# An attention and gated-scan kernel: the output projection in fp16 high and low parts, half a step to a step later

## The reference

```python
x = x + attn(layernorm(x))                  # per batch; inside attn: rms_norm, qkv = h @ w_qkv.T, rope on q and k
#   attn = softmax(mask(q k^T / 8)); out = attn @ v
#   return out @ w_out.T                    # [256,1024] @ [1024,128]: the output projection
z = layernorm(x)
for t in range(32):                         # the scan, c is [256,128]
    f = sigmoid(z[t] @ wf.T + c @ uf.T + bf);  i = sigmoid(z[t] @ wi.T + c @ ui.T + bi)
    g = tanh(z[t] @ wc.T + c @ uc.T + bc);     c = f * c + i * g
x = x + tanh(z @ wo.T + c @ uo.T + bo)
```

## Time and profile before

| | |
|---|---|
| median of 3 runs | 1133.13 us (1126.74 to 1135.27) |
| the profiled execution's own time | 1133.03 us |
| its span, first to last instruction | 1131.2 us |
| PE busy | 1080.3 us, 95% of the span |
| PE weight loads (PEld) | 813.6 us, 72% |
| DVE / ACT / POOL busy | 930.0 (82%) / 698.4 (62%) / 634.8 us (56%) |
| chain that ended last | PE 59%, DVE 16%, DMA 14% |
| granted TensorE clock, mean | 0.988 of 2.4 GHz |

### The profile page before, as it was taken

One profiled execution on the slowest core, in us unless ns is written; L12 is line 12 of the kernel. 1 busy time (PEld: TensorE's weight loads), 2 busy tenths in 40 slices (PEclk: granted clock), 3 DMA queues, 4 the chain that ended last, 5 costly groups with the idle time before them and its releaser, 6 DMA issues.

```text
span 1131.2 us, 47261 instructions
## 1 busy us (share of the span) xinstructions
PE 1080.3 (95%) x18443; PEld 813.6 (72%) x18443; DVE 930.0 (82%) x3305; ACT 698.4 (62%) x1575; POOL 634.8 (56%) x816
## 2 busy tenths in 40 slices
PE   3879999999999999999999999999999999999996
PEld 2457777777777776777777777677777777777784
DVE  5778888888888888888888888788888888888745
ACT  3556666666666666666666666666665666666644
POOL 3545665576565647656555665555565565556420
PEclk8889999999999999999999999999999999999999
DMA  6213343332333442233333233333323333332215
GB/s 204 95 62 112 111 115 114 115 95 89 111 111 114 115 114 90 90 111 115 115 115 115 83 100 115 107 114 115 115 78 98 114 115 111 108 112 92 68 36 150
DMA packets 78031, 120.52 MB, mean 107 GB/s; under 512 B 13041, under 2 KB 35954, under 8 KB 77682
## 3 DMA queue, kind: packets, MB, share of 16 engines
q1 hardware_dynamic: 68714, 111.20, 32.5%
q10 hardware_dynamic: 9096, 6.30, 2.1%
HBM read 41.56 MB, written 8.78 MB: 45 GB/s over the span
## 4 chain that ended last, share of the span: by engine, by line
PE 59%; DVE 16%; DMA 14%; SPq 4%; issue 3%; POOL 2%; ACT 1%; DVEq 0%; POOLq 0%
PE bank_pv L1142 11%; PE bank L1034 11%; DMA rope_c<-rope_b 10%; PE bank_st L1098 8%; PE bank_sum L1179 5%; PE bank_sum L1163 4%; DVE masked L809 4%; PE bank_sm L1073 4%; PE bank L1056 3%; DMA linv_scratch<-linv 3%; SPq L312 3%; DVE linv L832 2%; DVE rope_a L798 2%; PE bank L1281 2%; PE bank L1283 2%
## 5 line engine op out<-in xcount | busy, mean ns | idle before, releaser
L407 POOL TENSOR_TENSOR qk<-rope_a,rope_c 128x512 f32<-128x512 f32 x256 | 341.0, 1332 | 312.9 <-DMA rope_c<-rope_b 288.9
L809 DVE CUSTOM_DVE_ANT_0 masked<-bank_sm,mask_q 128x132 bf16<-128x132 f32 (+1 forms) x1024 | 307.1, 355 | 17.7 <-PE bank_sm L1073 17.2
L798 DVE TENSOR_TENSOR rope_a<-bank,cos 128x512 f32<-128x512 f32 x256 | 174.1, 680 | 130.1 <-PE bank L1034 83.7
L400 POOL TENSOR_TENSOR prob<-prob 128x264 f32<-128x264 f32 x256 | 210.8, 823 | 117.1 <-ACT prob L544 108.3
L529 ACT ACTIVATE qk_h<-qk 128x512 f16<-128x512 f32 x256 | 160.4, 627 | 172.2 <-POOL qk L407 171.7
L544 ACT ACTIVATE prob<-bank_st 128x784 f32<-128x784 f32 x256 | 209.3, 817 | 59.7 <-PE bank_st L1107 58.9
L1142 PE MATMUL bank_pv<-prob,v_sb 128*64 128x256 f32 (+1 forms) x2048 | 224.8, 340 | 0.6 <-DVE raw L825 0.6
L1098 PE MATMUL bank_st<-qk 64*64 64x256 f32 (+3 forms) x4096 | 186.3, 299 | 0.4 <-issue 0.2
L1098 PEld LDWEIGHTS bank_st<-qk 64*64 64x64 f32 x4096 | 167.7, 134 | 9.6 <-issue 1.3
L799 DVE TENSOR_TENSOR rope_b<-bank,sin 128x512 f32<-128x512 f32 x256 | 173.8, 679 | 0.0
L1142 PEld LDWEIGHTS bank_pv<-prob,v_sb 128*64 128x64 f32 x2048 | 124.3, 136 | 54.4 <-issue 0.9
(11 more groups left out here) (237 smaller groups left out, 1732.1 us busy)
## 6 DMA issues: line engine op xcount, KB each, us to landing
rope_c<-rope_b SPq DMA_DIRECT2D x512, 128.0 KB, 2.3
rinv<-linv_scratch SPq DMA_DIRECT2D x124, 256.0 KB, 4.8
out<-x_sb SPq DMA_DIRECT2D x16, 256.0 KB, 3.7
linv_scratch<-linv SPq DMA_DIRECT2D x62, 64.0 KB, 2.1
x_sb<-x ACTq DMA_DIRECT2D x28, 128.0 KB, 5.5
xt<-w_qkv_t ACTq DMA_DIRECT2D x1, 1024.0 KB, 5.3
v_end<-v_end_scratch SPq DMA_DIRECT2D x64, 8.0 KB
v_sb<-pm_v SPq DMA_DIRECT2D x63, 8.0 KB
```

The lines of the kernel that those rows point to most:

```text
L400: G.tensor_tensor(prob_2[:, s % 4, :, :], prob[:, s % 4, :, 0:NT - Q1], prob[:, s % 4, :, C0 + Q1:SCOL], ALU.add).then_inc(S["prob_added"], 1)
L407: G.tensor_tensor(qk[:, s, :].rearrange("p (u n) -> p u n", u=2)[:, :, 0:NT], rope_a[:, (NPAIR * j + s) % 3, :].rearrange("p (u n) -> p u ...
L798: V.tensor_tensor(rope_a[:, (NPAIR * j + s) % 3, :], proj_bank(j, s)[:, :], cos[:, :], ALU.mult)
L809: ins = V.tensor_tensor_reduce(masked[:, e, c0:c0 + n], ps_sm[:, e, c0:c0 + n], mask_q[:, c0:c0 + n], 1.0, LOWEST, ALU.add, ALU.max, top[: ...
```

## The change

`w_out` is kept as two fp16 matrices, `wo_hi` (the weights times 64, rounded) and `wo_lo` (what the rounding left). The normalised attention output is split in the same way into `y_hl`: ScalarE writes the high parts (`y_high`, a copy to fp16), GpSimd the low parts (`y_low`, a subtraction), a quarter of a batch at a time. `project_out` makes three fp16 matmuls (high by high, high by low, low by high) where one fp32 matmul was: 48 of 128 columns for a batch. The residual divides by 64. `y_hl` lies in the memory of `rinv`, so `spread_linv` now waits until the previous batch's projection is done.

The first half of the projection moves from step 5 to step 6, the second half from behind `project` in step 6 to the end of step 6. `residual`, `second_stats` move from step 6 to step 7, `second_norm` to step 0 of the next iteration, `transpose_xn` to the end of step 0 with its readers in step 1, `gates` to the ends of steps 1 and 2 and their `tanh` to steps 2 and 3. The last two batches keep a special order.

```diff
-        wo_sb = sb("wo_sb", [P, NPAIR, D], f32)
+        wo_hi = sb("wo_hi", [P, NPAIR, D], f16)
+        wo_lo = sb("wo_lo", [P, NPAIR, D], f16)
...
-        rinv = sb("rinv", [P, NPAIR, NT], f32)
+        y_hl = sb("y_hl", [P, 4, 2, 2 * NT], f16)
+        rinv = y_hl[:, :, :, :].rearrange("p n u m -> p (n u m)").bitcast(f32).rearrange("p (s n) -> p s n", s=NPAIR)
...
@@ SP, spread_linv
-                wait(sp, S["norm_done"], 4 * cj)
+                wait(sp, S["y_ready"], cj)
...
@@ POOL
+            def y_low(cj, par, n):
+                pool.wait_ge(S["y_hi_done"], 4 * cj + n + 1)
+                G.tensor_tensor(y_hl[:, n, 1, :].rearrange("p (s n) -> p s n", s=2), raw[:, par, 2 * n:2 * n + 2, :],
+                                y_hl[:, n, 0, :].rearrange("p (s n) -> p s n", s=2), ALU.subtract).then_inc(S["y_lo_done"], 1)
...
-                    if c and s == 7 and j < NB:
-                        rstd(j - 2)
+                    if s == 6 and c and j < NB:
+                        y_low(j - 2, p, 2)
+                        y_low(j - 2, p, 3)
...
                     if s >= 1 and a:
                         rope_add(j, s - 1)
+                    if s == 5 and c and j < NB:
+                        y_low(j - 2, p, 0)
+                        y_low(j - 2, p, 1)
+                    if s == 7 and c and j < NB:
+                        rstd(j - 2)
                     if b:
                         prob_add(j - 1, s)
...
@@ ACT
+                cast(A.activation(wo_hi[:, :, :].rearrange("p c d -> p (c d)"), o_raw, ACT.Copy, scale=WS))
...
+            def y_high(cj, par, n):
+                act.wait_ge(S["norm_done"], 4 * cj + n + 1)
+                A.activation(y_hl[:, n, 0, :].rearrange("p (s n) -> p s n", s=2), raw[:, par, 2 * n:2 * n + 2, :],
+                             ACT.Copy).then_inc(S["y_hi_done"], 1)
...
-                    elif s in (1, 2) and d and j - 3 < NB - 1:
-                        gate_tanh(j - 3, s - 1)
+                    elif s in (2, 3) and d and j - 3 < NB - 1:
+                        gate_tanh(j - 3, s - 2)
...
+                    if s == 5 and c and j <= NB:
+                        y_high(j - 2, p, 0)
+                        y_high(j - 2, p, 1)
                     if s == 5 and real(j + 1):
                         h_high(j + 1, 1 - p)
...
-                    if s == 7 and c and j < NB:
-                        second_norm(j - 2)
+                    if s == 0 and d and j <= NB:
+                        second_norm(j - 3)
...
@@ DVE
+                V.scalar_tensor_tensor(wo_lo[:, :, :].rearrange("p c d -> p (c d)"), o_raw, WS,
+                                       wo_hi[:, :, :].rearrange("p c d -> p (c d)"), ALU.mult,
+                                       ALU.subtract).then_inc(S["casts_dve"], 1)
...
+                    if s == 7 and c and j < NB:
+                        residual(j - 2)
                     if a:
                         rotate(j, s)
...
@@ PE, project_out
-                pe.wait_ge(S["norm_done"], 4 * cj + n + 1)
+                pe.wait_ge(S["y_lo_done"], 4 * cj + n + 1)
...
-                        last = T.matmul(y_out(cj)[:, q * D:(q + 1) * D], raw[:, par, s, q * P:(q + 1) * P], wo_sb[:, s, :],
...
+                        at = s % 2 * NT + q * P
+                        for i, (u, v) in enumerate(SPLIT):
+                            last = T.matmul(y_out(cj)[:, q * D:(q + 1) * D], y_hl[:, n, u, at:at + P], WO[v][:, s, :],
...
@@ PE, body
-                    if s in (5, 6) and c and j != NB:
+                    if s == 6 and c and j < NB:
+                        project_out(j - 2, p, 0)
+                        project_out(j - 2, p, 1)
+                    if s in (5, 6) and j == NB + 1:
                         project_out(j - 2, p, 2 * (s - 5))
                         project_out(j - 2, p, 2 * (s - 5) + 1)
...
+                    if s == 6 and c and j < NB:
+                        project_out(j - 2, p, 2)
+                        project_out(j - 2, p, 3)
                     if s in (2, 4, 7) and b:
                         sums(j - 1, (2, 4, 7).index(s))
+                    if s == 0 and d and j <= NB:
+                        transpose_xn(j, j - 3)
+                    if s in (1, 2) and d and j <= NB:
+                        gates(j, j - 3, s - 1)
```

More of the change, by code:

```diff
@@ L646, in body @@
                         load_batch(j + 4)
-                    if s == 0 and d and j != NB + 1:
+                    if s == (0 if j > NB else 1) and d and j != NB + 1:
                         xt_high(j - 3)
+                    if s == 1 and j == NB + 1:
+                        for n in range(4):
+                            y_high(j - 2, p, n)
                     if s == 1 and d and j - 3 == NB - 1:
                         gate_tanh_last(j - 3)
-                    elif s in (1, 2) and d and j - 3 < NB - 1:
-                        gate_tanh(j - 3, s - 1)
+                    elif s in (2, 3) and d and j - 3 < NB - 1:
+                        gate_tanh(j - 3, s - 2)
+                    if s == 3 and b:
+                        copy_top(j - 1, 1)
                     if s < 2 and j == 1:
@@ L691, in body @@
                         first_norm(j + 1)
+                    if s == 5 and c and j <= NB:
+                        y_high(j - 2, p, 2)
+                        y_high(j - 2, p, 3)
                     if s == 5 and d:
@@ L1310, in body @@
                             out_cf(g)
-                    elif s == 0 and d and j <= NB:
-                        transpose_xn(j, j - 3)
-                    if s in (1, 2) and d and j <= NB:
-                        gates(j, j - 3, s - 1)
                     if s == 1 and j == NB + 1:
```

45 lines of the change are left out of this document (28 added, 17 removed).

## The result

| | before | after |
|---|---|---|
| median | 1133.04 us (1126.74 to 1135.27, 4 runs) | 1273.81 us (1269.42 to 1278.04, 4 runs) |
| profiled execution, its own time | 1133.03 us | 1272.9 us |
| its span | 1131.2 us | 1271.1 us |
| granted TensorE clock, mean | 0.988 | 0.956 |

The ratio is 1.125 [1.119, 1.131]: the change makes the kernel 141 us slower. Forecast were 1300 us, between 1235 and 1335.

What follows compares the result with a forecast made beforehand. The prediction took PE to pace the iteration, busy 493.75 of 500 us. Profiled 1133.0 us plus 117 for the stall, 48 for the clock and 2 at the start gave 1300 us; range for 8 in 10, 1235 to 1335.

Steps and rivals of the forecast that it cites:

- The late `y_low`: On POOL, y_low queues behind the late rope_add of pair 3, prob_add and rope_add of pair 4; PE waits 3.5 us.
- The iteration walked through: The profiled iteration of the kernel before, 501.7 to 534.25 us, into whose queues the prediction put the new instructions.
- The price of `y_low`: Time of one y_low on GpSimd: 1.28 us, the median of L407, with bounds 0.75 and 1.71 us.
- The stall, 117 us: PE waits for low parts in step 6, so step 7 starts 3.9 us later in each of 30 iterations.
- The clock, 48 us: PE's waits in step 6 drop the clock to 1.2 GHz every iteration, costing 1.6 us each; 21 to 72 us.
- the stall without the clock: Rival, 24%: the stall comes as forecast but the clock stays at 2.4 GHz; 1252 us, 1220 to 1278.
- the early one of 4.26 us: PE wait ending at 67.17 us in the trace before; the clock fell to 0.5 from 65.6 to 72.4.
- the one of 2.67 us: PE wait near the end of the trace before, which brought no fall of the clock.
- PE's saving, 29 us: In the projection, 48 fp16 matmuls take 2.69 us against 3.67, relieving PE of 0.98 us a batch if it never waits.
- the rival "faster": Rival, 8%: the low parts come in time for PE; 29 us gained, 2 lost: 1106 us, up to 1125.
- The moved steps at nothing: Gates and second norm move with their readers; the third tanh costs 0 to 0.47 us an iteration, taken as 0.
- 1133 + 117 + 2 + 48: The 2 us: at the start DVE gets one more subtraction of 1024 elements where PE waits for DVE.

Runs made afterwards that it cites:

- E1: The changed kernel without the y_low subtraction; the projection waits for y_high and its third matmul rereads the high part, so the result lacks the low part: 1153.4 us.
- E4: The changed kernel with the first two quarters' y_high ahead of hi of pair 3 and their y_low ahead of rope_add of pair 3, in step 4: 1210.8 us.
- E8: The changed kernel with the spread of the inverse sums issued on SP behind the swap of pair 3, not ahead of it: 1290.6 us.
- E2: The changed kernel with 48 extra fp16 matmuls of a zero tile ahead of the projection's first half in step 6: 1235.2 us.
- E11: The kernel before with 48 fp16 matmuls on constant operands for the 16 fp32 ones, at the old places, nothing split, projection's result left out: 1126.0 us.
- E3: The changed kernel with the fp32 projection of the kernel before and no splitting, every step at its new place: 1158.7 us.
- E5: E3 with one thing put back: end_add ahead of rotate in step 1 on VectorE: 1152.7 us.
- E10: Control for E9: same places (first half in step 5, second at the end of step 6, end_add ahead of rotate), all fp32, nothing split: 1150.1 us.
- E9: The changed kernel with the projection's first half in fp32 back in step 5, only the second half split, in step 5, and end_add ahead of rotate: 1149.1 us.

## Why the prediction was right, point by point

**The late `y_low`: right.** The forecast had `rope_add` of pair 3 at 522.78 - 501.7 = 21.08 us into the iteration and `y_low` from 526.94 - 501.7 = 25.24; the medians after are 21.01 and 25.12. PE's wait for it was forecast at 3.5 us; the median is 3.16 over the 30 iterations. So close a hit is in part luck: the iteration walked through has an early swap, for before the change `rope_add` of pair 3 starts at 21.50 in the median, and the changed kernel has it 0.5 us sooner; why is open. E1 and E4 show that it is this wait, and that the place in POOL's and ACT's queues makes it. E8 shows that the swap is late because of the spread ahead of it. Curing either alone makes what is put behind it late (E4, E8).

**The price of `y_low`: a little high.** 1.28 us was taken from L407; its own line has a median of 1154 ns, which would have made the added wait 3.64 us an iteration instead of 3.92:

```profile
L417 POOL TENSOR_TENSOR y_hl<-raw,y_hl x124: 1142/1154/1612, 99.3 to 1224.2; 128x512 f16<-128x512 f32 x124
```

**The stall, 117 us: 102 measured (E2 less before, start included).** The position was right and the difference was not. The iteration walked through is 534.25 - 501.7 = 32.55 us long, and gave 32.55 + 3.92 = 36.47 without the clock; E2 has 36.40 in the mean and 36.13 in the median (the walk with 1154 ns for `y_low` gives 36.19). But the mean iteration before is 33.02 us, because in others the swap lands later and PE already waits for DVE, in 14 of 27 iterations for `top` and in 3 for `rotate` (step 7 starts at 28.86 us in the median, at 29.09 in the mean). 36.40 - 33.02 = 3.38 us, 30 times 101 us. An added wait has to be measured from the mean iteration where the waiting transfer scatters, and not from one in which nothing waits.

**The clock, 48 us: 39 measured (after less E2), 1.29 us an iteration.** That it falls nearly each time was right, in 29 of 30 iterations, and decided between the forecast and its strongest rival, the stall without the clock (1252 us). The reason given, that the wait is nearer in length to the early one of 4.26 us than to the one of 2.67 us, is not borne out. Two of the falls come where PE's waits in step 6 are only 0.7 (or 0.6), 1.38 and 0.72 us. E8 has waits of 1.85, 2.94 and 0.27 us in one iteration without a fall; it has a wait of 1.5 us or more in every iteration and a fall in 16 of 30. Its four runs took 1282, 1284, 1297 and 1299 us at mean granted clocks of 0.962, 0.968, 0.945 and 0.946. So it is in part luck that the falls came as regularly as forecast; what else decides is not shown. The size was too large: behind the early wait the level was low until 5.2 us after PE resumed; here the low stretch ends at 667.52, 3.84 us after 663.68.

**PE's saving, 29 us: wrong, and without effect on the sum.** In the prediction it decides only the rival "faster", which gives 1106 us. E11 has the whole saving with no stall of any kind, and reaches 1126. "PE is busy 494 of 500 us" was read as "PE sets the pace". E3, E5, E10 and E11 show what it hides: some of PE's work stood ahead of a wait for another engine and filled it, so PE was both busy and not needed that fast. Step 7 is held by the late swap and the 7.26 us of DVE's work behind it (E11). That rival would have been 1126 us at best, which is within the 1% called no change.

**The moved steps at nothing: wrong, hidden here.** Moved alone they cost 26 us (E3): `gates` covered `end_add`, the first half of the projection covered `rotate` of pair 5, and the second half covered `h_low` and `top` (E10). In the changed kernel they seem to cost nothing more (no run puts them back there one by one), since PE waits for `y_low` in any case, and the swap that decides when `y_low` starts is fixed to the start of the iteration, not to PE's step 5: step 5 starts 0.55 us later than before, `rope_add` of pair 3 does not. Had the low parts been in time, they would have been the loss: E1 has PE's saving and no low parts, and is 20 us slower than the kernel before.

The sum as measured: 1133 + 102 + 39 = 1274 us, against 1133 + 117 + 2 + 48 = 1300. Both large terms were too high, and the iteration takes 37.5 us where 38 to 39 were forecast.

No version with the whole computation beat the kernel before; the nearest is E9, 1.4% above. Whether the swap can be taken out of the spread's way without a new collision, by another queue for one of them, was not tried and stays open.

## What to carry to other kernels

Before you move or shorten work on a busy engine, ask what it stands in front of: work that fills a wait looks like a bound in the busy share, moving it costs the wait, and shortening it gains little (here 7 us of 29). New work on a helper engine is priced first by its place in that engine's queue, and so by what the queue waits for: here four subtractions of 1.15 us a batch cost 120 us in all (after less E1), because they stood behind one small transfer that lands behind 1 MB. And a wait of 3 us on TensorE was paid for once more, by 0.4 of its length, in the clock that fell with it in nearly every iteration.

## What the runs showed of the hardware that was not expected

- GpSimd's subtraction with one fp16 input and an fp16 output takes 1.15 us for 128x512, the addition with all fp32 of the same shape 1.28 us.
- The clock's falls come in 29 of the 30 iterations, for 3.4 us each, and mostly 37.55 us apart although the iterations take 36.3 to 38.4 us. With 48 matmuls of zeros, 2.84 us, in the wait (E2) one fall is left, though PE still waits for up to 0.5 us.
- The fp16 projection runs at the spacing that the tail of the kernel before had shown for this shape; its 48 weight loads add nothing that can be seen. In E2's timeline, twelve records of a quarter are started from 648.68 on within 0.62 us at the full clock:

```profile
648.68 0.23 PE L1233 MATMUL bank_sum<-wo_hi,y_hl 128*128 128x128 f16 x1 [0.49 <-POOL y_hl L419]
...
649.30 0.22 PE L1233 MATMUL bank_sum<-wo_hi,y_hl 128*128 128x128 f16 x1
```

- A swap of two transfers of 128 KB, issued 2.6 us behind the start of a 1 MB spread on the same queue, lands so much later that its reader starts 3.7 us later than when it is issued ahead of it (21.01 against 17.27 us, after and E8). From issue to landing it takes 6.0 us in the median after the change; the swaps of pairs 1, 2, 5 and 6 take 2.6.
